# List scatters in new places in the pass, and the LayerNorm shift made by VectorE instead of GpSimd

## What is computed

```python
x = x + attention(layernorm(x))          # q, k = elu(.)+1; scans of k*v and of k over time
...
logits = xf @ router_w.T + router_b
top_vals, top_idx = top_k(logits, 4)
rw = softmax(top_vals) * 1.8
routed = sum over the 4 chosen experts e of rw * (silu(xf @ gate_w[e].T) * (xf @ up_w[e].T)) @ down_w[e].T
x = x + routed + shared                  # xf = layernorm(x); experts of width 192
```

## Time and profile before

| | |
|---|---|
| median of 3 runs | 662.66 us (661.18 to 666.01) |
| the profiled execution | 662.23 us, its span 660.5 us |
| PE busy | 578.3 us (88%) |
| DVE busy | 479.9 us (73%) |
| ACT busy | 471.1 us (71%) |
| POOL busy | 438.2 us (66%) |
| list scatters (line 589) | 128, 136.9 us busy |
| chain that ended last, by engine | PE 53%, POOL 13%, DVE 9%, DMA 9%, issue 9% |

### The profile page before, as it was taken

How to read it: one execution, slowest core, us unless ns; L and a number is a source line. 1 busy time by engine, 2 the same in 40 slices (tenths; PEclk the granted TensorE clock), 3 DMA queues, 4 the chain that set the end, 5 groups by cost and what they waited for, 6 DMA issues and landing times.

```text
span 660.5 us, 15988 instructions
## 1 busy us (share of the span) xinstructions
PE 578.3 (88%) x4909; PEld 409.2 (62%) x4909; DVE 479.9 (73%) x1907; ACT 471.1 (71%) x1138; POOL 438.2 (66%) x359
## 2 busy tenths in 40 slices
PE   4899999899898979999999999999999999998000
PEld 2476676476575557777777777777777777775000
DVE  3569999899979887776666666666666666665163
ACT  4778887769776458897888888788888888787000
POOL 3033177888888877752888888788888788788100
PEclk9999999899999999999999999999999999999555
DMA  8945687879786799976888888898998888886799
GB/s 332 337 147 181 223 261 247 285 265 328 242 265 209 263 288 307 341 265 178 146 141 146 142 143 140 141 147 136 147 146 143 143 140 142 140 140 75 251 409 381
DMA packets 102070, 140.43 MB, mean 213 GB/s; under 512 B 15522, under 2 KB 87746, under 8 KB 101442
## 3 DMA queue, kind: packets, MB, share of 16 engines
q1 hardware_dynamic: 69424, 97.28, 45.9%
q0 software_dynamic: 29040, 38.68, 34.7%
q10 hardware_dynamic: 3522, 3.44, 1.7%
HBM read 79.19 MB, written 64.89 MB: 218 GB/s over the span
## 4 chain that ended last, share of the span: by engine, by line
PE 53%; POOL 13%; DVE 9%; issue 9%; DMA 9%; SPq 3%; ACT 3%; POOLq 0%; ACTq 0%; DVEq 0%
PE psD L1356 13%; PE psQ L1325 12%; PE psK L1325 12%; POOL xlist_scratch L589 8%; PE psT L1296 5%; DMA acc_scratch<-arena 5%; SPq L518 3%; DMA W<-acc_scratch 2%; PE psT L1347 2%; PE psV L1347 2%; PE psD L1413 2%; POOL rstd L574 2%; POOL W L567 1%; POOL acc_scratch L636 1%; DVE stats L843 1%
## 5 line engine op out<-in xcount | busy, mean ns | idle before, releaser
L636 POOL DMA_INDIRECT acc_scratch<-arena x159 | 250.5, 1575 | 72.7 <-ACT arena L692 37.9
L589 POOL DMA_INDIRECT xlist_scratch<-list_row,dest x128 | 136.9, 1069 | 38.6 <-issue 35.9
L1356 PE MATMUL psD<-W,arena 128*128 (+1 forms) x955 | 135.5, 273 | 0.0
L1141 DVE COPY arena<-psT 128x512 f16<-128x512 f16 x191 | 81.0, 424 | 67.2 <-PE psT L1296 65.6
L1325 PE MATMUL psK<-W,arena 128*128 (+1 forms) x576 | 109.3, 326 | 0.7 <-DVE arena L1141 0.7
L1325 PE MATMUL psQ<-W,arena 128*128 (+1 forms) x570 | 108.2, 326 | 0.1
L1356 PEld LDWEIGHTS psD<-W,arena 128*128 128x128 f16 x955 | 85.4, 98 | 6.8 <-ACT arena L680 0.3
L683 ACT ACTIVATE arena<-arena 128x192 f16<-128x192 f32 x191 | 69.2, 362 | 12.0 <-DVE arena L1163 0.6
L692 ACT ACTIVATE arena<-psD,arena 128x256 f32<-128x256 f32 x159 | 73.1, 459 | 6.3 <-DMA acc_scratch<-arena 5.8
L1296 PEld LDWEIGHTS psT<-ident,arena 128*128 128x128 f16 x764 | 58.0, 98 | 25.9 <-issue 2.1
L1296 PE MATMUL psT<-ident,arena 128*128 128x128 f16 x764 | 73.9, 219 | 0.0
(11 more groups left out here) (185 smaller groups left out, 1085.9 us busy)
## 6 DMA issues: line engine op xcount, KB each, us to landing
arena<-xlist_scratch SPq DMA_DIRECT2D x159, 136.0 KB
arena<-in_w_early_dram SPq DMA_DIRECT2D x24, 640.0 KB, 4.9
W<-acc_scratch SPq DMA_DIRECT2D x24, 512.0 KB, 12.6
acc_scratch<-arena SPq DMA_DIRECT2D x16, 512.0 KB, 8.9
arena<-in_L_attn_x_dram SPq DMA_DIRECT2D x10, 512.0 KB, 5.8
xlist_scratch<-pad_scratch SPq DMA_DIRECT2D x32, 136.0 KB
list_row<-xrow_scratch SPq DMA_DIRECT2D x32, 136.0 KB
acc_scratch<-arena SPq DMA_DIRECT2D x33, 128.0 KB, 15.2
```

The costliest lines, as they stand in the source:

```text
L589: nc.gpsimd.indirect_dma_start(xlist[:, :], bass.IndirectOffsetOnAxis(ap=dest[:, n:n + 1], axis=0), list_row[j % LISTS][:, :], None).then_ ...
L636: nc.gpsimd.indirect_dma_start(acc[t % ACCS][:, :], bass.IndirectOffsetOnAxis(ap=token[:, (t - NT) % DEEP:(t - NT) % DEEP + 1], axis=0), y ...
L1141: nc.vector.tensor_copy(xT[t % 2].rearrange("p s c t -> p (s c t)"), psX[t % 2]).then_inc(xT_done, 1)
L1356: last = nc.tensor.matmul(psY[u], aT[u][0:height, part], weights(t - 2, GUW + q * H, H, height), start=(n == 0), stop=(n == len(parts) - 1))
```

## The change

`LIST_FROM` goes from 15 to 14 scatters a step: steps 3 to 8 have 14 each, and 44 instead of 39 remain for the tile phase. `FETCHED` follows from it. In POOL's step one scatter now stands ahead of the first root, six between the roots, and the other seven between the second root and the value products; behind the products there are none. The shift leaves POOL: DVE makes it with one `scalar_tensor_tensor`, (mean * -1) * rstd, where it made the negated mean before (`norm_less`, line 858 before), and waits for the first root there.

```diff
-        LIST_FROM = [0, 0, 0] + [15 * n for n in range(NB - 2)] + [89]
+        LIST_FROM = [0, 0, 0] + [14 * n for n in range(NB - 1)]
...
                 nc.gpsimd.tensor_tensor(rstd[n][:, :], vare[n][:, :], mhalf[:, :], ALU.pow).then_inc(ln_rstd[n], 1)
-                if n == 0:
-                    pool.wait_ge(ln_less, b + 1)
-                    pool.wait_ge(ln_rstd[0], b + 1)
-                    nc.gpsimd.tensor_tensor(shift, less, rstd[0][:, :], ALU.mult).then_inc(ln_shift, 1)
...
+                if b >= 3:
+                    list_some(0, 1)
                 if st.after:
                     root(0, b + 1)
                 if b >= 3:
-                    list_some(0, 4)
+                    list_some(1, 7)
                 if st.past:
                     number_rows(b - 2)
                 if st.before:
                     root(1, b - 1)
                 if b >= 3:
-                    list_some(4, 5)
-                if b >= 3:
-                    list_some(5, 12)
+                    list_some(7, 20)
                 if st.now:
                     kv_sum_product(b, 0)
                     kv_sum_product(b, 1)
-                list_some(12 if b >= 3 else 0, 20)
...
             def norm_vare(n, b):
                 if n == 0 and b >= 1:
-                    dve.wait_ge(ln_shift, b)
+                    dve.wait_ge(ln_rstd[0], b)
...
-            def norm_less(b):
+            def norm_shift(b):
+
+                dve.wait_ge(ln_rstd[0], b + 1)
                 if b >= 1:
-                    dve.wait_ge(ln_shift, b)
-                dve.wait_ge(ln_aggr[0], TS * b + TS)
-                nc.vector.tensor_tensor(less, mv[0][:, :, 0], minus_words[:, :], ALU.mult).then_inc(ln_less, 1)
+                    dve.wait_ge(xn_ready, TS * b)
+                nc.vector.scalar_tensor_tensor(shift, mv[0][:, :, 0], -1.0, rstd[0][:, :], ALU.mult, ALU.mult).then_inc(ln_shift, 1)
```

More of the change, by code:

```diff
@@ L109, in moe_block @@
         rden = carve(TS * HEADS)
-        less = carve(TS)
         shift = carve(TS)
@@ L189, in moe_block @@
         eps_words = sb("eps_words", [P, TS], f32)
-        minus_words = sb("minus_words", [P, TS], f32)
         stats = [sb(f"stats{n}", [P, TS, 6], f32) for n in range(2)]
@@ L231, in moe_block @@
         ln_rstd = [sem(f"ln_rstd{n}") for n in range(2)]
-        ln_less, ln_shift = sem("ln_less"), sem("ln_shift")
+        ln_shift = sem("ln_shift")
         ln_words_made = sem("ln_words_made")
@@ L849, in norm_vare @@
                 if n == 0 and b >= 1:
-                    dve.wait_ge(ln_shift, b)
+                    dve.wait_ge(ln_rstd[0], b)
                 wait_apart(dve, ln_aggr[n], TS * b + TS, 2 + n)
                 nc.vector.tensor_tensor(vare[n][:, :], mv[n][:, :, 1], eps_words[:, :], ALU.add).then_inc(ln_vare[n], 1)
-            def norm_less(b):
+            def norm_shift(b):
+                dve.wait_ge(ln_rstd[0], b + 1)
                 if b >= 1:
-                    dve.wait_ge(ln_shift, b)
-                dve.wait_ge(ln_aggr[0], TS * b + TS)
-                nc.vector.tensor_tensor(less, mv[0][:, :, 0], minus_words[:, :], ALU.mult).then_inc(ln_less, 1)
+                    dve.wait_ge(xn_ready, TS * b)
+                nc.vector.scalar_tensor_tensor(shift, mv[0][:, :, 0], -1.0, rstd[0][:, :], ALU.mult, ALU.mult).then_inc(ln_shift, 1)
             nc.vector.memset(eps_words[:, :], LN_EPS).then_inc(ln_words_made, 1)
-            nc.vector.memset(minus_words[:, :], -1.0).then_inc(ln_words_made, 1)
-            dve.wait_ge(ln_words_made, 2)
+            dve.wait_ge(ln_words_made, 1)
             dve.wait_ge(x_loaded[0], 16)
@@ L865, in _ @@
             norm_vare(0, 0)
-            norm_less(0)
+            norm_shift(0)
             for n, which in enumerate(QKV_ORDER):
@@ L985, in step @@
                 if st.after:
-                    norm_less(b + 1)
+                    norm_shift(b + 1)
                 if st.now:
```

## The result

The changed kernel takes 678.06 us, the median of 4 runs (677.56 to 679.29). The kernel before, run beside it, takes 663.75 us (median of 4, 661.18 to 666.01). The ratio is 1.020, with an interval of 1.016 to 1.025: the change makes the kernel 2% slower. The forecast was 672.6 us with a range of 665 to 678. The sign is right; the number is 5.5 us too low and the median lies just outside the range, by 0.06 us.

A forecast was written before the change was run, and what follows sets the result against it. POOL was taken to bound steps 4 to 7, PE the routed tiles. Late list rows end the last scatter 10.3 us later; less 0.4 slack, +10.0 on 662.23 gives 672.2, plus 0.4 for the median: 672.6 us, range 665 to 678.

The forecast's parts named there:

- E3: End of POOL's two value products in step 3, the later ones numbered likewise by step; forecast 118.4 us, not 112.2.
- E7: End of POOL's two value products in step 7; forecast 225.1 us against 217.4, moving the tile phase by 7.7 us.
- Step 3: POOL's thirteenth scatter waits 7.7 us for list row 3 ahead of the value products, which end at 118.4 us.
- Steps 5 and 7: POOL's thirteenth scatter waits 5.9 and 2.8 us for list rows 10 and 17, taken to land 4.2 and 3.8 us after issue.
- Steps 4 and 6: Passes of 25.5 us, with 1.5 us each (between 0 and 2.2) for PE's low clock in the projection after its longer wait.
- The shift on DVE: DVE waits 0 to 0.3 us for the first root; POOL saves 0.86 us a pass.
- The tail: After step 7's products, 20.1 us to the first paced scatter, then 44 scatters at 1.295 us; last ends 10.3 us later.
- The seam: From shared to routed tiles: the end of the list work has 0.4 us of slack, leaving +10.0 us in all.
- rival (d): PE's clock falls oftener, also in step 8 and at the seam, 1.8 us each: 676 us; chance 0.12.
- (a): List rows are there in time for POOL's scatters; the end of the scatters binds, 8.6 us earlier: about 654 us; chance 0.06.
- (b): List rows land about 2.4 us after issue, so POOL's waits are together 5.7 us less: 667 us; chance 0.12.
- (c): PE's low clock costs nothing, since DVE sets passes 4 and 6: 3.0 us less, 669.6 us; chance 0.15.

## Why the prediction was right, and where its size was off

**What bounds, and by what mechanism: right.** The forecast was that the thirteenth scatter would wait for rows 3, 10 and 17 ahead of the products, for 7.7, 5.9 and 2.8 us; it waited 7.83, 7.49 and 3.85. That these waits are the cause is shown by the run with three rows at the head, on the first chip: without them 13 of 14 us are gone. That the products hold attend and with it the projection is in the rows at 116.63 and 117.97.

**The ends, step by step.**

| | forecast | measured | before |
|---|---|---|---|
| E3 | 118.4 | 116.53 | 112.19 |
| E4 | 143.9 | 142.49 | 140.03 |
| E5 | 173.8 | 174.19 | 165.95 |
| E6 | 199.3 | 200.32 | 192.40 |
| E7 | 225.1 | 228.24 | 217.39 |
| last scatter ends | 301.9 | 307.02 | 291.58 |
| first load from the lists | 305.8 | 309.80 | 295.52 |

*Step 3*, 1.9 us early: 1.2 of it is the second root, which came at 96.24 and not at 97.4, since the passes before it gained 1.7 us that I had not counted (step 2's products end at 84.01 against 85.72). The rest is a row that landed 0.3 us sooner after the root and two scatters that took 2.3 us instead of 2.55.

*Steps 5 and 7*, 1.8 and 2.1 us too short (31.7 for 29.9, 27.9 for 25.8): two terms of the sum were mis-sized. The landings were taken as 4.2 and 3.8 us, from "fewer pads ahead" and a queue that had all but drained; they were 5.4 and 4.9, no shorter than row 3's 5.1. And rows 7 and 14, loaded at the end of steps 4 and 6, were not in the sum at all. They are late too (0.97 and 1.83 us), and they put off the scatters and the roots of the next step: the second root came 11.8 and 11.6 us after the products' end where I had 10.8 and 9.95.

*Steps 4 and 6*: 25.96 and 26.13 for 25.5, so the 1.5 us for the low clock was about right, a little low (up to 1.7 and 1.9 on this chip, 0.9 to 1.1 to the root on the other). Its upper bound, "2.2 (both projections at half speed)", does not follow from the rows: both projections took 3.88 us before, and at half speed they would take as much again; the trace shows 2.6 us more. Only part of that reached the root.

*The shift on DVE*: "0 to 0.3 us of waiting" was right, no idle time ahead of it at 119.25. It rested on the root with one scatter ahead of it, which the prediction counted. With three ahead the same edit costs 6 us, and my own expectation of that run, a gain, had forgotten it.

*The tail*: 20.7 us for 20.1 to the first paced scatter. The 44 scatters took 58.1 us for 56.7; the difference is one pause of 1.92 us, which the profile puts down to a turned tile. I had 0 to 0.5 us for pacing.

**The seam: the step that failed.** I counted only the shift of the list's end, less 0.4 us of slack. PE arrives there 10.9 us later and the first load 14.3 us later, and the difference is not only waited for (3.3 us) but followed by matmuls at half the clock, together some 2.6 us more than the load's own shift less the slack (16.5 - 13.9). That was the seam half of rival (d), which I gave 0.12 and a total of 676; its other half, a low clock in step 8, did not come (PE idled 0.41 us there, clock 1.00). The first load came only 2.8 us behind the end of the last scatter, where I had the 3.9 of before, which hid 1.1 of the 5.1 us by which the scatters ended later than forecast. Adding up: the first load was 4.0 us later than forecast, the seam cost those 2.6 more, and that is nearly all of the 6.7 us between the forecast span of 670.5 and 677.2.

**The other rivals.** (a), rows in time, fell with the first wait. It also put that case at 654, and the run that is this case by its edit took 665: the bound it named, the end of the scatters, did bind, but the last one ended at 289.3 us and not at 283.0: E7 came at 209.4 for 206.2, and POOL paused twice in the tile phase, for 2.1 and 1.2 us, until a tile was turned. (b), shorter waits, fell: its landings of 2.4 us are half of those of the three rows (5.1, 5.4 and 4.9 us), and even with no pad of the step ahead they took 4.5 and 5.5 us. The estimate of 2.3 us in the prediction is worked out from the Trainium skill ("DMA: Bandwidth & Descriptors", section "Anatomy of one DMA"), which gives these figures for a DMA issued by GpSimd; here SP issues the loads. It met the shortest of the 32 list row loads of the changed kernel (2.3 us) and missed the three that matter. (c), the clock costs nothing, fell with the 26.0 and 26.1 us of passes 4 and 6 against 24.2 in the run whose clock stayed up.

## What to carry to other kernels

Before a consumer is moved up in an in-order queue, look up when its input is *produced*: here twelve scatters of a pass found their rows loaded, and the thirteenth took the products, and with them two other engines, behind a load that its own queue issues last. Moving an instruction to another engine moves its wait too; ask what stands behind it there, and make the producer early first. And where two chains meet with little slack, an imbalance of three microseconds can cost more than three: here TensorE waited 3.3 us and then went on at the low clock.

## What the runs showed of the hardware

- The late list rows, loads of 128 rows, landed 4.5 to 5.5 us after their issue, nearly the same with six, five and no pad copies of 136 KB in front of them. Over all 32 of these loads in the changed kernel (line 440) the time spreads further, as the line below shows. What sets it was not tried by itself.

```profile
DMA to landing us min/median/max: 2.3/4.3/6.7
```

- The granted clock was 0.50 from 117 to 123 us around the end of an idle time of 3.96 us in step 4, and below 1.00 from 314 to 318 behind two waits of 1.40 and 1.94 us at the seam. A wait of 0.60 us ahead of the same projection in the kernel before left it at 1.99 us for eight matmuls.
- An idle time of the same length did not always end in the same clock: after 1.45 us ahead of the same six 128x512 matmuls in step 7 the clock stayed at 1.00 in the kernel before (209.97), and was 0.50 for some 10 us (213 to 223) in the run with the shift on DVE alone.
- Two chips differ by 6% on the same program (664 and 704 to 706 us). On the second one PE is busy for 54.0 of 75 us in the shared tiles, against 64.4 of 70 on the first, and the DMA engines move 229 GB/s there against 289:

```profile
245.00:320.00 75.00, 54.03 (x436) 34.83 (x434) 42.53 (x156) 36.82 (x96) 45.28 (x47) 0.93 0.73 229
```

```profile
245.00:315.00 70.00, 64.36 (x590) 46.03 (x588) 53.57 (x200) 53.34 (x146) 46.04 (x48) 1.00 0.88 289
```

The first of these rows is the changed kernel on the second chip, the other the changed kernel on the first. At its 0.93 the clock explains little of it. Engines wait there for what the profile calls "remote" (DVE 18.7 us in 255 to 340), and why that chip is slower stays open. A loss of 2.0% on one chip was 1.5% on the other, with intervals that overlap.
